# A transformer block on one core: per-batch vector work moved to a table over score tiles, output projection summed in PSUM

## The reference

```python
mod = (_silu(L0_c) @ L0_wmod).reshape(L0_c.shape[0], 6, 1, -1)
sa, ca, ga, sb, cb, gb = (mod[:, 0], mod[:, 1], mod[:, 2], mod[:, 3], mod[:, 4], mod[:, 5])
ga = (2 * (ga >= 0) - 1) * jnp.maximum(jnp.abs(ga), 0.25)
...
h = _layernorm(x, axis=-1) * (1 + ca) + sa
x = x + ga * _L0_attn_ref(h, ...)       # q, k, v; causal softmax of q.k + q.position; @ v; @ out_kernel + out_bias
h = _layernorm(x, axis=-1) * (1 + cb) + sb
x = x + gb * _L0_ffn_ref(h, ...)        # softmax gate, argmax expert, place = running count, relu MLP, times gate
```

## Time and profile before

| | us |
|---|---|
| median of 3 runs | 977.36 |
| lowest, highest | 976.86, 979.02 |
| span of the profiled execution, first to last instruction | 967.2 |
| what lies around the span (median less span) | 10.2 |
| PE busy | 877.3 (91% of the span) |
| DVE, ACT, POOL busy | 738.3, 713.5, 517.3 |
| mean granted clock of PE | 0.967 |

### The profile page before, as it was taken

How to read it: one execution, slowest core, us unless ns; L and a number is a source line. 1 busy time by engine, 2 the same in 40 slices (tenths; PEclk the granted TensorE clock), 3 DMA queues, 4 the chain that set the end, 5 groups by cost and what they waited for, 6 DMA issues and landing times. The chain is left out here.

```text
span 967.2 us, 20244 instructions
## 1 busy us (share of the span) xinstructions
PE 877.3 (91%) x5455; PEld 688.3 (71%) x5455; DVE 738.3 (76%) x2166; ACT 713.5 (74%) x1969; POOL 517.3 (53%) x767
## 2 busy tenths in 40 slices
PE   4799999999999999999999999999999999963894
PEld 3577777777767767776778676776777777732894
DVE  6687788787887788887878788778878787852685
ACT  3688887887868787877888787887788878831452
POOL 3355555556556644665555555664466556532354
PEclk8899999999999999999999999999999999985998
DMA  7069000000000000000000000000000000025661
GB/s 234 1 174 242 1 1 12 2 2 34 1 12 0 34 1 11 1 9 25 12 1 1 25 1 12 0 19 1 11 1 7 14 12 1 2 69 165 195 201 53
DMA packets 31403, 38.62 MB, mean 40 GB/s; under 512 B 2998, under 2 KB 25975, under 8 KB 31056
## 3 DMA queue, kind: packets, MB, share of 16 engines
q1 hardware_dynamic: 27760, 30.08, 11.1%
q0 software_dynamic: 3072, 5.94, 1.7%
q10 hardware_dynamic: 480, 1.70, 0.5%
HBM read 23.37 MB, written 16.82 MB: 42 GB/s over the span
## 5 line engine op out<-in xcount | busy, mean ns | idle before, releaser
L391 POOL TENSOR_SCALAR prob<-prob,rsum 128x128 f32<-128x128 f32 (+3 forms) x512 | 267.1, 541 | 286.4 <-DVE rsum L1010 286.2
L510 ACT ACTIVATE prob<-srow,nmax 128x512 f32<-128x512 f32 (+3 forms) x512 | 286.6, 560 | 117.7 <-DVE nmax L998 116.0
L998 DVE CUSTOM_DVE_ANT_0 srow<-bank,consts 128x512 f32<-128x512 f32 (+3 forms) x512 | 247.4, 489 | 105.9 <-issue 58.4
L718 PE MATMUL bank<-consts,prob 128*128 128x128 f32 x1280 | 203.8, 274 | 0.2 <-POOL prob L391 0.2
L710 PE MATMUL bank<-khi,qhi 128*128 128x512 f32 (+2 forms) x384 | 150.7, 392 | 30.2 <-DVE nmax L998 16.9
L718 PEld LDWEIGHTS bank<-consts,prob 128*128 128x128 f32 x1280 | 159.1, 141 | 25.5 <-DVE pt L1006 2.4
L384 POOL TENSOR_TENSOR qlo<-qx,qhi 128x384 fp32r<-128x384 f32 x128 | 129.7, 1014 | 64.5 <-ACT qhi L499 64.4
L519 ACT ACTIVATE pt<-bank 128x384 f32<-128x384 f32 x318 | 155.3, 497 | 9.6 <-PE bank L718 8.7
L738 PE MATMUL bank<-pt,v 128*64 128x512 f32 (+3 forms) x1024 | 151.9, 439 | 0.6 <-issue 0.6
L710 PE MATMUL bank<-khi,qlo 128*128 128x512 f32 (+2 forms) x384 | 130.2, 339 | 0.0
L710 PE MATMUL bank<-klo,qhi 128*128 128x512 f32 (+2 forms) x384 | 129.7, 338 | 0.0
(11 more groups left out here) (173 smaller groups left out, 1462.2 us busy)
## 6 DMA issues: line engine op xcount, KB each, us to landing
x<-xbuf SPq DMA_DIRECT2D x17, 385.0 KB, 3.2
xbuf<-fill SPq DMA_DIRECT2D x4, 1540.0 KB, 21.7
raw<-in_L_ffn_W SPq DMA_DIRECT2D x16, 256.0 KB, 9.0
prob<-in_L_ffn_W SPq DMA_DIRECT2D x16, 256.0 KB, 4.4
out<-row SPq DMA_DIRECT2D x8, 256.0 KB, 2.3
raw<-in_L_attn_qkv ACTq DMA_DIRECT2D x3, 512.0 KB, 5.6
modb<-mod_rows SPq DMA_DIRECT2D x1, 1536.0 KB, 7.6
v<-in_L_ffn_b SPq DMA_DIRECT2D x1, 1024.0 KB, 7.0
```

The lines of the kernel that those rows point to most:

```text
L391: end = gp.tensor_scalar(part, part, rsum[:, par, 4 * h + q:4 * h + q + 1], 1.0, ALU.mult, ALU.mult)
L510: act.activation(prob[:, par, h, QOFF[q]:QOFF[q] + P * (q + 1)], srow[:, k % 4, 0:P * (q + 1)], ACT.Exp, bias=nmax[:, par, k:k + 1], scale ...
L718: last = pe.transpose(out[:, n * P:(n + 1) * P], prob[:, par, h, QOFF[q] + k * P:QOFF[q] + (k + 1) * P], ident)
L998: dve.tensor_tensor_reduce(out=srow[:, k % 4, 0:w], in0=scb[k % 2][:, 0:w], in1=mask[:, S - w:S], scale=-1.0, scalar=BIG, op0=ALU.add, op1 ...
```

## The change

It touches only the attention part and the helpers once per batch.

- **A table instead of lists.** `before_attention` and `after_attention` name the pair (a, k) after which each part runs on DVE. `stats1`, `stats2`, `xhat1`, `xhat2` take a range of tiles and run in two halves.
- **`moments` becomes `aggregate`:** four `bn_aggr` per use; adding epsilon moves to POOL (`root`), ahead of the power.
- **`accumulate` and `acc` are gone.** `project_out` keeps adding in the bank `opb` over the eight steps of a batch (`start` only for a = 0, `stop` only for a = 7). `residual` reads `opb`, adds the bias and multiplies in one instruction.
- **The PE helpers** `turn_x`, `turn_a`, `turn_h`, `logits`, `places` write `xtb`, which is `prb[1]`. Each waits until ACT has read V out of that bank, and q head 1, the last projection of the step, waits for the reader of the helper's result. `turn_a`, `turn_h`, `logits`, `places` come a step sooner (`turn_a` and `turn_h` at k = 5), `turn_x` too.
- **ACT:** `normed` from step 3 to 2, `second` from (4, 4) to (3, 6), `gates` from step 5 to 4. **POOL:** the second power follows `divide` in step 2, it was ahead of it in step 3; `gated` goes from step 6 to 5; the four scatters (the "stores" of routed rows) go two to step 6 and two to step 7. `xn` has a tile of its own.

```diff
@@ POOL @@
+            def root(i, n):
+                waits(gp, ("pch", 1), (f"rst{i + 1}", n))
+                gp.tensor_scalar(vare[:, i, :], mom[:, i, :, 1], EPS, None, ALU.add).then_inc(s[f"va{i + 1}"], 1)
+                gp.wait_ge(s[f"va{i + 1}"], n)
+                gp.tensor_tensor(rstd[:, i, :], vare[:, i, :], mhalf[:, :], ALU.pow).then_inc(s[f"rs{i + 1}"], 1)
...
                         if a == 6:
+                            scatter(b, (0, 1))
                         if a == 7:
-                            scatter(b)
+                            scatter(b, (2, 3))
                     divide(j, a % 2, 0)
+                    if not first and a == 2:
+                        root(1, b)
@@ PE @@
             def project_out(j, a):
                 pe.wait_ge(s["ol"], j + 1)
-                wait(pe, "ac", j)
                 for i, (w, o) in enumerate(((wohi, ohi), (wohi, olo), (wolo, ohi))):
-                    last = pe.matmul(opb[:, :], w[:, a, :], o[:, :], start=(i == 0), stop=(i == 2))
+                    last = pe.matmul(opb[:, :], w[:, a, :], o[:, :], start=(a == 0 and i == 0),
+                                     stop=(a == PAIRS - 1 and i == 2))
...
+                    if (a, k) == (2, 4) and not last:
+                        pe.wait_ge(s["ve"], j + 4)
+                        turn_x(b + 1)
+                    if (a, k) in ((1, 5), (3, 5), (4, 4), (5, 4)) and not first:
+                        pe.wait_ge(s["ve"], 8 * B if last and a >= 5 else j + 4)
+                        (turn_a, None, turn_h, logits, places)[a - 1](b)
...
                 if after:
+                    if a == 2 and not last:
+                        pe.wait_ge(s["hn"], b + 2)
+                    if a in (1, 3, 4, 5) and not first:
+                        pe.wait_ge(s[("x2", None, "hh", "lge", "prx")[a - 1]], b)
                     project_q(j + 1, n, m, 1, 8 * B if last and V_OF[a][0] else j + 4)
@@ DVE @@
+            def aggregate(i, n):
+                for q in range(QT):
+                    end = dve.bn_aggr(mom[:, i, q, :], stats[:, i, q, :])
+                end.then_inc(s[f"rst{i + 1}"], 1)
...
-                dve.tensor_scalar(hn[:, :], acc[:, :], modT[:, 4, bass.ds(b - 1, 1)], None, ALU.mult)\
+                dve.tensor_scalar(hn[:, :], opb[:, :], bo[:, 0:1], modT[:, 4, bass.ds(b - 1, 1)], ALU.add, ALU.mult)\
...
-                    parts[0] = [lambda: stats1(n), *moments(0)]
-                    parts[2] = [lambda: xhat1(n)]
-                    parts[4] = [lambda: low(n)]
-                    parts[1] = [None, lambda: residual(b)]
-                    parts[2] = [lambda: residual2(b), lambda: stats2(b), *parts[2], *moments(1)]
-                    parts[3] = [None, lambda: xhat2(b)]
-                    parts[5] = [lambda: gating(b), lambda: choice(b), None, lambda: gate_of(b)]
-                    parts[6] = [lambda: place(b), lambda: route(b), lambda: index(b)]
```

More of the change, by code:

```diff
@@ L333, in _ @@
             gp.wait_ge(s["pch"], 1)
-            rstd(0, 1)
+            root(0, 1)
             gp.wait_ge(s["w_k"], 16)
@@ L964, in _ @@
             stats1(0)
-            for part in moments(0):
-                part()
+            aggregate(0, 1)
             dve.wait_ge(s["wv"], 1)
```

226 lines of the change are left out of this document (107 added, 119 removed), and 6 rows, old and new, of the table names.

## The result

| | before | after |
|---|---|---|
| median of 4 runs, us | 977.13 | 936.57 |
| lowest, highest | 976.86, 979.02 | 934.02, 937.23 |
| span of the profiled execution | 967.2 | 932.2 |
| mean granted clock of PE | 0.967 | 0.975 |

The ratio is 0.9583, with an interval of 0.9564 to 0.9603: 40.6 us faster. The forecast was 950.4, its range 943.5 to 961.0. What is worth learning is that 24 us of the 27 were forecast step by step and came as 26.5, and that most of the rest lies where the forecast did not look closely: in the one execution that it took as its basis, and in the scatters, which it dismissed on the word of that execution.

What follows compares the result with a forecast made beforehand. PE bounds the kernel, busy 91% of the span. 22.6 + 3.9 + 1.9 + 0.57 + 0.2 - 2.2 = 27.0 us off the 967.2 us span, with 10.2 around it, gives 950.4 us; range 943.5 to 961.0.

Steps and rivals of the forecast that it cites:

- the 10.2 us around it: Time outside the profiled span of 967.2 us, up to the median of 977.4, carried over unchanged into the forecast.
- PE did not wait for either, so nothing is gained: Moving two of four scatters from step 7 to POOL's idle time in step 6 was priced at no gain.
- `moments` at the start of step 3: Seven DVE instructions ahead of the first score tile; moving them gains 2.99 us per batch, plus 3.9 for three clock falls.
- The rival that they would be held up like L935: `bn_aggr` is long: at 0.96 us each the gain is eaten, at 1.2 the kernel takes 991 us; chance 0.04.
- `residual`'s read of PSUM: Two readings per batch: 0.26 us slower by the single rate, 0.24 faster by the loop's row; only the tail's 0.26 counted.
- behind the branch: Step 0 after the branch back: DVE starts 2.44 us late; 0.45 us charged in each of five batches, 2.2 in all.
- `x2`: New PE wait before step 1's last projection, the one with least room: `residual2` late, charged 0.25 us per batch.
- step 7's 0.65 us: `place`, `route`, `index` ahead of `klo` make PE wait; moved to step 5, they take the wait to step 6: gain 0.
- Start and tail: Tail: 0.57 us from dropping `accumulate` and `residual` reading PSUM. Start and tail's `aggregate`: 0.2 us.
- that rival: The clock falls again behind PE waits, losing 3.9 us and up to 6.5 more: 957 us, chance 0.12.
- The new waits of PE: `x2`, `hh`, `low` and the late `root` cost 0.6 us each in seven batches: 965 us, chance 0.08.
- better than summed: Under 944 us, with no price behind the branch and `x2` free; chance 0.03.

Runs made afterwards that it cites:

- experiment 12: The kernel before, unchanged, profiled and timed again on a third chip: 977.67 us.
- experiment 6: The kernel after with its scatters not split, all four in step 7: 942.01 us, 0.9662 of before.
- 10 to 12: Together on a third chip: after unchanged 935.38 us, after with all four scatters in step 7 940.38 us, before unchanged 977.67 us.
- 2x2: Four variants of after: seven instructions at the old place 962.68 us, in the table 947.90; `bn_aggr` at the old place 935.63, in the table 936.57.
- experiment 8: The kernel after with `accumulate` put back behind score tile 3 and `xn` sharing `xh` again: 945.89 us, 0.9697 of before.
- experiment 13: The kernel after with its loop over batches 1 to 6 written out, no branch back: 917.86 us, 0.9411 of before.
- experiments 2 and 3: 2: before with four `bn_aggr` in place of `moments`, epsilon on POOL, 947.68 us. 3: after with the seven instructions at the table's places, 947.90 us.
- experiment 9: The kernel before with `accumulate` adding only 4 of 512 columns, same 64 instructions and waits: 967.35 us against 968.49 on the second chip.
- experiment 5: The kernel after with the second layernorm's four `bn_aggr` behind `evac_q` ending step 2, its power on POOL in step 3: 935.63 us, second chip.
- experiments 1 and 7: 1: before unchanged, 976.32 us. 7: before with scatters writing 4 elements per row to a small buffer, routed rows left out, 975.14 us.
- experiment 4: The kernel after with seven instructions for the second layernorm behind `evac_q` ending step 2, its power on POOL in step 3: 962.68 us.

## Why the prediction was wrong, point by point

**The basis: "the 10.2 us around it".** This is the step that failed first. The runs on record have 1.8 us around their spans (2.2 in two kernels). A profiled execution that lies 8.4 us under the median is not a typical one, and the difference was the largest unexplained figure of the case. The trace of experiment 12 shows what it lacked: its span is 8.6 us longer, 6.5 in step 7, 0.8 ahead of the first `weighted`, 1.2 behind the last. After's own execution was 2.6 us under its median: it had a mean clock of 0.975, its three other runs 0.971 or 0.972, in which part is not on record. So of the error of 13.8 us, 5.8 are here (10.2 carried over, 4.4 measured) and 8.0 in the sum: 2.2 in batches 1 to 6, 1.2 in batch 7, 2.6 in start and tail, 2.8 in the experts' part, less 0.8 in batch 0.

**"PE did not wait for either, so nothing is gained"** (the scatters). True of the one execution that was read, false of the runs that were timed. Worth 5.4 and 5.0 us in experiments 6 and 10 to 12. This is what the 8.4 us were made of for the most part: 6.5 to 6.8 us of stalls in step 7. So this step and the one above are one error seen from two sides: the time of the stalls was taken for a constant around the span, which the change could not touch, and the change took it away.

**`moments` at the start of step 3.** The size was right: 2.99 us per batch forecast, 3.1 measured, and the three falls of the clock went as priced (3.9). The cause was given by halves. I tied it to the place, and the 2x2 shows that the kind of instruction suffices. `bn_aggr` was taken at 0.2 us, four at 0.8. Four of them in step 2 of batch 2, beside POOL's `divide`:

```profile
258.68 2.08 POOL L395 TENSOR_SCALAR prob<-prob,rsum 128x128 f32<-128x128 f32 x4 [3.82 <-DVE rsum L1007]
...
260.13 0.38 DVE L933 BATCH_NORM_AGGREGATE mom<-stats 128x2 f32<-128x6 f32 x4
```

0.38 us for four. None of the 64 took over 0.182 alone. The rival that they would be held up like L935 in the earlier trace rows fell, though POOL was not idle there, as the forecast had argued. The Trainium skill's rule that was quoted (VectorE: DVE Perf Modes, "Two Vector instructions with no wait between them"), that one input doesn't use the shared read interface, agrees with this row.

**`residual`'s read of PSUM.** It takes 0.81 us in each of the eight batches, where the forecast had 0.75. That is 0.32 us more than L1046 took alone and 0.17 less than its mean, so both of the forecast's readings had the right sign. At its new place no instruction of POOL runs beside it; before, `qlo` (L384) did in the loop.

**The steps.** Forecast for steps 1, 2, 3, 4, 6 and 0 behind the branch: 12.3, 12.5, 12.3, 12.8, 12.4, 14.6. Measured: 12.25, 12.29, 12.19, 12.69, 12.46, 14.34 in the mean of five. The sum for batches 1 to 6 was 24.3 us (22.6 + 3.9 - 2.2), measured 26.5. What is over are small charges that were not due: `x2` (0.25 a batch), `low` (0.1), the late `root` (0.1), and behind the branch 0.12 in place of 0.45 (14.22 in the mean before). These are more than the 2.2; against them, of the 0.25 of step 6 only 0.1 came: steps 6 and 7 took 24.9 us together, what is now steps 5 and 6 takes 24.8, and steps 1 and 2 keep a few hundredths each. That `x2` was near the edge is shown by experiment 8. The reading of step 7's 0.65 us, as the price of nine instructions in front of `klo`, was wrong: experiment 13 shows for the same parts in their new step that most of it belongs to the loop.

**Batch 7, batch 0.** 3.1 us against 1.9: I subtracted its small waits, which didn't come. Batch 0 lost 0.8 and was put at 0: `modulation` with `xhat1` behind it in step 1 makes `klo` late by 1.5 us, against gains in the steps before. It was within the bounds given.

**Start and tail.** 0.8 us forecast (0.57 + 0.2), 3.4 measured. Where nobody works beside DVE, what counts is the chain: seven linked instructions against four that follow one another at 0.1 us. For the start, experiments 2 and 3 bear this out: 51.06 us with `bn_aggr` in before, 54.64 with the seven in after. In the tail it is one part of two: the stretch of 24.97 us takes 26.39 with the seven instructions, and 25.83 with `accumulate` (experiment 8), which was priced at 0.57 and cost 0.86. The tail in after (start, us, engine, what, idle before):

```profile
834.29 0.38 DVE L933 BATCH_NORM_AGGREGATE mom<-stats 128x2 f32<-128x6 f32 x4
...
834.84 0.24 POOL L331 TENSOR_SCALAR vare<-mom 128x4 f32<-128x4 f32 x1 [10.62 <-DVE mom L933]
...
835.16 1.04 POOL L333 TENSOR_TENSOR rstd<-vare,mhalf 128x4 f32<-128x4 f32 x1
```

0.24 us for epsilon on POOL was priced at 0.2.

**`accumulate`.** Right for the steps of the kernel before (experiment 9). But a thing that costs nothing where it stands may still be what a new layout cannot hold: 9.3 us in the table (experiment 8). The parts don't add up for that reason: `bn_aggr` alone 28, the split 5, `accumulate` 9, together 42 of 40.6.

**The rivals.** The clock did not fall in the steps of the two traces of after. But the argument against that rival, that behind the branch's wait of 1.29 us it never fell, does not hold: it fell once or more behind that branch in experiments 2 to 6, in one to three batches of five, also in kernels that differ from after in one place only (15.63 us in experiment 6, 15.49 and 15.48 in experiment 5). The new waits of PE did not come. `bn_aggr` was not long. The case that I gave 0.03, better than summed, was the one that came, and its reasons ("no price behind the branch, `x2` free") were the smaller part of it.

## What to carry to other kernels

Before a sum is made on one profiled execution, compare its time with the spread of the timed runs; if it lies outside, the trace lacks something that the runs have, and an item that costs nothing in it (here a burst of four scatters beside a busy DVE) may be just that. Small linked instructions on a few elements are priced by their chain and by who holds them up, not by their number times their duration: replace them by one instruction before moving them. And work that is free in a slack layout is to be priced again in the packed one.

## What the runs showed of the hardware

- Beside four indirect scatters in a row on POOL, 0.97 to 1.24 us each, DVE stands idle for 0.5 to 1.8 us, in the step shown with its input complete, and in the stalled steps compared of experiments 1 and 7 ACT starts 0.7 to 0.9 us late; on two chips of three, with 50 GB/s or with 1 GB/s moved. With two in a row, where they stand in after, there is no such surplus. Which resource it is, why one chip shows none, and why DVE sometimes starts only 0.8 us after the last scatter, is open.
- Four `bn_aggr` of 128x6 take 0.38 us, beside POOL's work too; seven linked instructions on 128x4 in their place cost the kernel 11 us more in the table and 27 more at the old place.
- A branch back costs DVE 2.4 us and PE 1.2 to 1.6 of wait, 2.4 us of the step's length, and this was the largest item left: 12 of the 18.7 us that the written-out loop gave.
- Behind the same wait of PE the granted clock may fall to 1.2 GHz or stay at 2.4: in step 3 it fell in two batches of six behind a longest wait of 1.48 us (experiment 4), and behind 1.37 to 1.39 us in 3, 1, 3, 2 and 0 of six (the traces of the earlier trace rows and of experiments 1, 12, 7 and 9). A fall cost 1.2 to 1.3 us.
